# The encoder layers' norms: a third token tile of 40 tokens in place of an overlapping 128

## What is computed

```
def _ln(x, g, b, eps=1e-05):
    m = jnp.mean(x, axis=-1, keepdims=True)
    v = jnp.mean((x - m) ** 2, axis=-1, keepdims=True)
    return (x - m) * jax.lax.rsqrt(v + eps) * g + b
...
for l in range(LAYERS):
...
    o = o @ Wo[l].T + bo[l]
    x = _ln(x + o, ln1_g[l], ln1_b[l])
    ff = jax.nn.gelu(x @ W1[l].T + b1[l], approximate=False) @ W2[l].T + b2[l]
    x = _ln(x + ff, ln2_g[l], ln2_b[l])
```

## Time and profile before

| | |
|---|---|
| time, median of 3 runs | 821.56 us (820.96 to 822.18) |
| span of the profiled execution, first to last instruction | 819.1 us |
| granted TensorE clock, mean over the span | 1.000 of full speed |
| busy: PE, PEld | 801.5 us (98%), 751.4 us (92%) |
| busy: DVE, ACT, POOL | 633.9 (77%), 460.6 (56%), 251.6 us (31%) |
| chain that ended last | PE 47%, issue 23%, POOL 18%, DVE 8% |

### The profile page before, as it was taken

How to read it: one execution, slowest core, us unless ns; L and a number is a source line. 1 busy time by engine, 2 the same in 40 slices (tenths; PEclk the granted TensorE clock), 3 DMA queues, 4 the chain that set the end, 5 groups by cost and what they waited for, 6 DMA issues and landing times.

```text
span 819.1 us, 16629 instructions
## 1 busy us (share of the span) xinstructions
PE 801.5 (98%) x6060; PEld 751.4 (92%) x6060; DVE 633.9 (77%) x1287; ACT 460.6 (56%) x829; POOL 251.6 (31%) x297
## 2 busy tenths in 40 slices
PE   9999999999999999999999999999999999999988
PEld 8998789999999999899999989999998999999758
DVE  5786693778778876778797887878778787876796
ACT  4386424433333336585786777667687767745421
POOL 0002120410111100364366147335525623633020
PEclk9999999999999999999999999999999999999999
DMA  5010946998889812010210021031012103010001
GB/s 191 1 52 1 373 124 253 328 323 310 317 309 337 321 53 107 1 40 14 100 44 0 17 98 38 13 102 38 4 39 72 38 13 102 26 82 1 1 0 30
DMA packets 18290, 88.36 MB, mean 108 GB/s; under 512 B 3120, under 2 KB 7472, under 8 KB 12240
## 3 DMA queue, kind: packets, MB, share of 16 engines
q1 hardware_dynamic: 18256, 87.90, 30.4%
HBM read 85.05 MB, written 2.84 MB: 107 GB/s over the span
## 4 chain that ended last, share of the span: by engine, by line
PE 47%; issue 23%; POOL 18%; DVE 8%; ACT 3%; DMA 1%; POOLq 0%; SPq 0%; DVEq 0%; ACTq 0%
PE bank L1139 14%; POOL W_L L2000 7%; PE bank L1176 6%; POOL HF_L L2058 4%; POOL arena L1981 3%; POOL WQKV_L L2000 3%; PE bank L746 2%; PE bank L872 2%; PE bank L1185 2%; PE bank L722 2%; PE bank L1049 2%; PE bank L788 1%; POOL SQ L2019 1%; PE bank L1123 1%; PE bank L1490 1%
## 5 line engine op out<-in xcount | busy, mean ns | idle before, releaser
L1139 PE MATMUL bank<-arena 128*128 (+1 forms) x1024 | 117.8, 274 | 0.0
L1139 PEld LDWEIGHTS bank<-arena 128*128 128x128 f32 x1024 | 117.4, 192 | 0.0
L1981 POOL TENSOR_TENSOR arena<-arena,srec 111x456 f32<-111x456 f32 x56 | 52.3, 962 | 125.1 <-DVE srec L2153 125.1
L2000 POOL TENSOR_TENSOR W_L<-LW,W_H 128x256 fp32r<-128x256 f32 x96 | 68.5, 752 | 36.9 <-DVE XHL L2589 33.5
L2058 POOL TENSOR_TENSOR HF_L<-arena,HF_H 128x296 fp32r<-128x296 f32 x48 | 43.8, 937 | 76.7 <-ACT HF_H L1896 76.7
L788 PE MATMUL bank<-XHL,W_H 128*128 128x296 f32 x288 | 65.1, 307 | 0.0
L1896 ACT ACTIVATE arena<-bank,vec 128x296 f32<-128x296 f32 x96 | 48.8, 509 | 20.4 <-PE bank L788 15.4
L2012 POOL TENSOR_TENSOR QW<-QW,arena x14 | 22.4, 1600 | 119.0 <-DVE QW L2490 65.6
L1330 PE MATMUL bank<-HF_L,W_H 128*128 128x296 f32 x192 | 57.4, 299 | 0.0
L1330 PE MATMUL bank<-HF_H,W_H 128*128 128x296 f32 x192 | 57.4, 299 | 0.0
L1330 PE MATMUL bank<-HF_H,W_L 128*128 128x296 f32 x192 | 57.3, 299 | 0.0
(11 more groups left out here) (276 smaller groups left out, 2205.4 us busy)
## 6 DMA issues: line engine op xcount, KB each, us to landing
arena<-ew_in SPq DMA_DIRECT2D x16, 2048.0 KB, 9.0
arena<-ew_in SPq DMA_DIRECT2D x16, 1024.0 KB, 7.0
LW<-lw_in SPq DMA_DIRECT2D x12, 1024.0 KB, 5.0
arena<-route SPq DMA_DIRECT2D x32, 185.0 KB, 3.2
LW<-lw_in SPq DMA_DIRECT2D x6, 768.0 KB, 4.3
fp_weights<-arena SPq DMA_DIRECT2D x1, 2048.0 KB, 6.4
arena<-fp_weights SPq DMA_DIRECT2D x1, 2048.0 KB, 7.2
arena<-patches_in SPq DMA_DIRECT2D x2, 864.0 KB, 7.4
```

The costliest lines, as they stand in the source:

```text
L1139: last = mm(o[:, m * CAP:(m + 1) * CAP], w[:, kc, mi * P:(mi + 1) * P], xg(kc, e), start=(kc == 0), stop=(kc == C - 1))
L1981: nc.gpsimd.tensor_tensor(v, v, srec[0:QROWS, s:s + 2, :].unsqueeze(3).to_broadcast([QROWS, 2, C * JH, KEYS]), ALU.mult).then_inc(p_ready, 1)
L2000: last = nc.gpsimd.tensor_tensor(low[:, cols], value[:, cols], high[:, cols], ALU.subtract)
```

## The change

The layers' norms (those whose sequence is a tuple) get the tiles of 128, 128 and 40 tokens, without overlap; the other norms (tokens, block 0, experts, encoder entry, final) and the patch statistics keep tiles of 128 that overlap. Where the third tile has 40 tokens, the variance product has 40 stationary columns and writes 40 partitions, and the broadcast transpose has 40 rows of weights (`ln_rs[0:40]`, still repeated to 128 columns), the 40 x 40 corner of the identity as moving operand and 40 columns of output. Nothing changes in the number or the order of the instructions, on no engine; ScalarE and VectorE still handle 128 partitions x 3.

```
-            return (0, P), (P, P), (nt - P, nt - 2 * P)
+            return (0, P), (P, P), (nt - P, P)
+
+        def norm_tiles(seq):
+
+            nt = ln_geometry(seq)[1]
+            return ((0, P), (P, P), (2 * P, nt - 2 * P)) if isinstance(seq, tuple) else var_tiles(nt)
...
-                for t, (t0, _) in enumerate(var_tiles(nt)):
+                for t, (t0, n) in enumerate(norm_tiles(seq)):
                     for c in range(nch):
                         at = VAR_AT + t * VAR_W
-                        last = mm(ln_bank(seq, h)[:, at:at + VAR_W], sq[:, h, c, t0:t0 + P], ones[:, 0:VAR_W],
+                        last = mm(ln_bank(seq, h)[0:n, at:at + VAR_W], sq[:, h, c, t0:t0 + n], ones[:, 0:VAR_W],
                                   start=(c == 0), stop=(c == nch - 1))
...
-                nt = ln_geometry(seq)[1]
                 pe.wait_ge(ln_rstd, ln_count(seq, h))
-                for t, (t0, _) in enumerate(var_tiles(nt)):
-                    last = nc.tensor.transpose(ln_bank(seq, h)[:, t0:t0 + P], ln_rs[:, h, t:t + 1].to_broadcast([P, P]),
-                                               ident)
+                for t, (t0, n) in enumerate(norm_tiles(seq)):
+                    last = nc.tensor.transpose(ln_bank(seq, h)[:, t0:t0 + n], ln_rs[0:n, h, t:t + 1].to_broadcast([n, P]),
+                                               ident[0:n, 0:n])
```

## The result

| | before | after |
|---|---|---|
| median of 5 runs, us | 821.56 (820.96 to 822.18) | 827.11 (826.88 to 827.46) |
| ratio, 95% interval | | 1.0070 (1.0059 to 1.0081) |
| span of the profiled execution, us | 819.1 | 825.1 |

The change makes the kernel slower by 5.55 us, at a granted clock of 1.0 in both. The direction is the forecast one, the size is over three times the forecast 1.7 us, and the time lies above the range.

A forecast was written before the change was run, and what follows sets the result against it. TensorE, busy in 98% of the span, was taken as the bound. First and last odd phases -0.05, four odd +0.12, five even +1.50, last phase -0.025 and +0.17 gave +1.7 us: 823.3 us, range 821.2 to 826.1.

The forecast's parts named there:

- Bound and place: TensorE, busy in 98% of the span, bounds; changes at the two edited calls pass through its waits for VectorE.
- s1: First norm's broadcast transpose: the 40-row load's standstill delays TensorE's next instruction by +0.19 us.
- s2: Second norm's broadcast transpose: the standstill and an unhidden load delay TensorE's next line by +0.275 us.
- b: Broadcast transpose: the broadcast itself is done +0.08 us later.
- v: Variance product: both third-tile passes shrink from 0.11 to 0.055 us, -0.105 us a norm.
- the prediction's own sign of being wrong: Listed signs: third broadcast load starts early, variance loads show an idle of their own, or odd phases grow as even ones.
- the load sets the pace: Variance product: loads follow each other in 0.11 us and set the pace; a 40-column load should fit into 0.055.
- In the second norm v goes: Second norm: VectorE's nine evacuations set the reciprocal, so the variance's -0.105 us vanishes in TensorE's wait, 0.17 and 0.105 more.
- never late: Odd phases: VectorE's chain from the second norm to RSUM takes no delay from the edits.
- RSUM's wait gives way: Odd phases, mean product: 0.22 us of waiting for RSUM absorbs part of the 0.275 delay, leaving +0.055.
- The fourth score's wait: Fourth score product: 0.20 us of waiting covers TensorE's +0.14 in odd phases; even phases give back 0.06.
- The second rival: Variance product stalls too: +0.115 us in place of -0.105, odd phases +0.25, even +0.52, 4.4 us, 826.0; chance 0.10.

The follow-up runs named there:

- the broadcast alone: Against the kernel after: variance product's third tile back to 128 columns, broadcast transpose kept at 40 rows; 823.98 us, 1.0035 of the kernel before.
- the kernel with 64: Against the kernel after: third tile of 64 tokens from 232 on in both forms, 24 tokens done twice; 827.79 us, 1.0080 of the kernel before.

## Why the prediction was wrong in size

**Bound and place: right.** TensorE is busy in 98% of the span, and the time is lost at the two edited calls and carried on through the waits named.

**The broadcast: right.** 0.17 of idle ended by "issue", the line behind it 0.185 and 0.26 us later for the forecast s1 = 0.19 and s2 = 0.275. The broadcast is done 0.07 us later (forecast b = 0.08). With the broadcast alone, the even phases and the four odd ones between them came to within 0.05 us of the prediction's terms.

**The variance product, v = -0.105: the step that failed.** It measured +0.157, and the prediction's own sign of being wrong, an idle of the variance's loads, is there. The prediction took "the load sets the pace" to hold down to 40 columns, and weighed against the stall the transposes of the earlier trace rows, 64 columns with no idle. Those rows have the size but not the operation: they are transposes, the variance product is not, and at 64 columns it stands still (1.6 us in 24 norms) where they do not (0.0). They have 128 moving columns, too, where the variance product has 64, and no run separates the two differences; why these transposes are spared stays open. That it is the change of form that costs shows in the two loads of each norm: the first load of 40 columns has 0.067 us of idle, the second, of the same form, none.

The Trainium skill (TensorEngine Tiling (Array Packing), Tiling Modes, Key Properties) says that a change of the tiling mode drains TensorE. The idle of 0.067 us before the 40 columns and of 0.17 before the 40 rows fits that. The Trainium skill (same page, Overview) calls a dimension of 64 or less small; here 64 pays and 65 does not. The Trainium skill (same page, Restrictions) shuts fp32 transposes out of column tiling. The earlier trace rows fit that as well; no run here tests it, nor shows that a mode changes.

**"In the second norm v goes": wrong as well, though the reciprocal was read rightly.** VectorE comes to it when it has done its nine evacuations, as the prediction says, and TensorE's wait there does swallow the variance's delay (with the short variance in second norms alone, the broadcast comes 0.11 us less late than the first value product before it). What was overlooked is the work queued behind the variance on TensorE: eight value products, and behind those VectorE's last three evacuations, which had nothing to spare. So VectorE's chain, "never late", is late by 0.15 at the projection and at RSUM.

**RSUM's wait gives way: right while RSUM is on time.** With the broadcast alone, odd phases keep 0.10 us. In the kernel after RSUM itself is 0.15 late, and the wait gives back only the rest.

**The fourth score's wait: right.** Behind it TensorE is late by 0.11 to 0.13 us less in odd phases, 0.09 of which in five of the six come already at the products of line 788 (now 792) just ahead: in the kernel before a load there waited 0.05 to 0.07 us for the subtraction, too, and no longer does. In even phases it is late by 0.06 less, as forecast, but most of that is lost again within 4 us, and 0.02 remain.

**The sum with the measured terms.** Even phase: 0.26 + 0.157 + 0.185 - 0.02 = 0.58, measured 0.60. Odd phase, by VectorE's chain: 0.15 at RSUM + 0.157 + 0.07 = 0.38, measured 0.37. The second rival, the variance product stalls too, is what happened; it gave 826.0 with 0.25 and 0.52 a phase. Its own price of 0.115 up to the next line was measured as 0.107. (Its parts add up to 0.46, not 0.45, so the price should have read 0.125.) It fell short by the 0.05 that the unhidden load behind adds, and by the second norm's evacuations: 6 x 0.12 + 5 x 0.08 = 1.1 us, about the difference to 827.1.

## What to carry to other kernels

Before a tile is cut to its remainder, look whether the remainder falls to 64 or fewer rows or columns of weights: here that turned a gain of 2.2 us (65) into a loss of 6.5 (64). Three like tiles of 99 beat both the overlapping and the remainder tile. To price a form from a trace, take a row of the same operation, not only of the same shape; and when a wait seems to hide a delay, follow all that is queued behind the late instruction, not only the wait's own chain.

## What the runs showed of the hardware that was not expected

- An fp32 product with 64 or 40 stationary columns among ones with 128 makes TensorE stand still, 0.067 us ahead of the first of two such loads and 0 ahead of the second, and with what it does to the lines behind it costs 0.157 us a norm at 40 columns; with 65 columns there is no idle. For transposes with 64 or 40 rows the idle is 0.17 us, with 65 rows none.
- The idle doesn't depend on how small the form is: 1.6 and 4.1 us at 40 and at 64. The rest of the price grows a little with the form: at 64 columns the third tile's second pass starts 0.107 us behind the first (0.087 at 40), and the line behind the third transpose starts 0.196 behind it (0.176). Odd phases are 0.43 longer than before and even ones 0.63, where 40 tokens gave 0.37 and 0.60. That makes 6 x 0.06 + 5 x 0.03 = 0.5 of the 0.7 us by which the kernel with 64 is slower than the one with 40 (827.79 and 827.11).
- Above the limit the pace of the variance's passes follows the columns of the load: 0.059 us at 65, 0.065 at 72, 0.087 at 99, 0.112 at 128.
